# Writing out the loop over the six layers on every engine

## The chip, the cores and the metric

The kernel runs on one core of one Trainium2 chip. The metric is the time on the device of one execution, in microseconds (us), as the median of three runs. One more execution was recorded by the hardware profiler; its rows are in the section ahead of the prediction. TensorE is called PE in them (PEld is its weight load), VectorE DVE, ScalarE ACT, GpSimd POOL, SyncE SP.

## The reference, cut to what matters

Four blocks follow each other, each on the layer-normed stream, with the result added back: causal attention with 16 heads, a gated low-rank mixture of experts, chunked retention, and a transformer of six layers. The last is where the change is and where most of the time goes:

```
for layer in range(6):
    x = x + attn_layer(shift_tokens(x), Wqkv[layer], ...)   # 16 heads of 64, window 32, l2norm, rotary with scales
    x = x + ffn_layer(shift_tokens(x), W1[layer], ...)      # layer norm, 128 -> 2*341, a * gelu(gate), 341 -> 128
```

Here x has 16 sequences of 256 tokens of 128 numbers, all in float32.

## The kernel before

Each engine has a program of its own, and they meet in semaphores. The function `layers` holds the six layers. On each engine `one_layer(layer)` issues one layer, and a hardware loop runs it six times with `layer` in a register, for instance `with pe.Fori(0, DEPTH) as layer` (line 1259; 1013 on POOL, 1402 on DVE, 1542 on ACT, 930 on SP). So each engine has the code of one layer once and branches back to its head five times.

Within a layer there are two parts.

**The window attention** is a software pipeline over 16 sequences x 4 steps (two tiles of 128 tokens, two halves of the heads). `pipeline` writes out the four steps of sequence 0, runs sequences 1 to 14 in an inner hardware loop of 14 passes (line 899), and writes out sequence 15 and four steps of draining. A step on PE is, in this order: project keys (L1095), turn queries (L1103), project queries (L1095), turn keys (L1103), turn probabilities (L1128), values (L1115), scores (L1173, 64 small matmul passes), values (L1115), apply probabilities (L1154, some 28 small ones). ACT squares the projections (L1450, L1458), DVE rotates them (L1320), POOL adds (L979) and scales (L995) the rotated halves, and PE turns them in the next step.

**The MLP** goes over eight chunks of 512 tokens: the first are interleaved with the draining steps, then comes an inner hardware loop (line 911) of three passes with two chunks each, and the last chunk is written out. L1074 is the up projection, L1083 the down projection, ACT's L1425 the gelu, DVE's L1302 the product and L1309 the addition to the stream.

The end of a layer already does work for the next: SP has loaded the next attention weights, PE fuses them (L1025), ACT and DVE take the fused weights (L1410, L1271), DVE makes the rotation tables (L1265). Then the head of the next layer begins: on PE with waits on the fused weights and on the shifted tokens `w_xs` (ACT L1432), and with `project(1)`, L1095.

Waits are on counts that grow over the whole run, such as `passed(layer * N + seq * STEPS + ...)`. Where `layer` or `seq` is a register, register instructions work the count out ahead of the wait.

Of the kernel before, what the change touches and what calls it, by code (L numbers as in the profile page):

```python
# [40 lines left out]
DEPTH, WH, WD, WIN = 6, 16, 64, 32  # L41
# [26 lines left out]
def passed(count):  # L68
    return count + 1
# [772 lines left out]
def layers(nc, sem, sb, h, xT, spare0, spare1, banks, ident, wqk, wv, wo, base, scl, tab, mask, w1, w2, col):  # L842
# [64 lines left out]
    def finished(layer, c):  # L907
        return passed(layer * NCH + NCH + c)
# [18 lines left out]
    with nc.Block() as block:  # L927
        @block.sync
        def _(sp):
            with sp.Fori(0, DEPTH) as layer:  # L930
                sp.wait_ge(M["residual"], finished(layer, 0))
                sp.sem_inc(sem("gate"), 1)
                sp.wait_ge(S["u_made"], passed(layer * N * 2 + N))
                sp.sem_inc(sem("gate"), 1)
                for dst, name in ((w1, "m_w1"), (w2, "m_w2"), (col, "m_col")):
                    sp.dma_start(dst[:], h[name][bass.ds(layer, 1)].squeeze(0)).then_inc(S["mlp_weights"], 16)
                sp.wait_ge(S["u_made"], passed((layer + 1) * N * 2))
                sp.sem_inc(sem("gate"), 1)
                sp.wait_ge(S["tabled"], passed(layer + 1))
                sp.sem_inc(sem("gate"), 1)  # L940
                sp.wait_ge(M["residual"], finished(layer, 2))
                sp.sem_inc(sem("gate"), 1)
                load_window_weights(sp, S["weights"], h, (layer + 1) % DEPTH, wqk, wv, wo, scl)

        @block.gpsimd
        def _(pool):
# [63 lines left out]
                        shift_chunk(i * 2 + k, k)  # L1010
                        invert(i * 2 + k)

            with pool.Fori(0, DEPTH) as layer:
                one_layer(layer)

        @block.tensor
        def _(pe):
            def fuse(turn, part):
                for par in range(2):
                    if part == 1:  # L1020
                        pe.wait_ge(S["fused_taken0"], passed(turn * 2 + par + 1))
                        pe.sem_inc(sem("gate"), 1)
                    rows = slice(64 * par, 64 * par + 64)
                    for g in range(NPAIR):
                        last = nc.tensor.matmul(fused_bank(par)[:, g], wv[rows, part * NPAIR + g, :],  # L1025
                                                wo[rows, part * NPAIR + g, :], start=True, stop=True)
                    last.then_inc(S["fused"], 1)
# [228 lines left out]
            pe.wait_ge(S["weights"], 64)  # L1256
            fuse(0, 0)
            fuse(0, 1)
            with pe.Fori(0, DEPTH) as layer:
                one_layer(layer)  # L1260

        @block.vector
        def _(dve):
# [4 lines left out]
            def take_fused(turn):  # L1268
                for par in range(2):
                    dve.wait_ge(S["fused"], passed(turn * 4 + 2 + par + 1))  # L1270
                    nc.vector.tensor_copy(fused_weights(par, 1), fused_bank(par)).then_inc(S["fused_taken1"], 1)  # L1271
# [127 lines left out]
            dve.wait_ge(S["weights"], 64)  # L1399
            tables()  # L1400
            take_fused(0)
            with dve.Fori(0, DEPTH) as layer:
                one_layer(layer)

        @block.scalar
        def _(act):
            def take_fused(turn):
                for par in range(2):
                    act.wait_ge(S["fused"], passed(turn * 4 + par + 1))
                    nc.scalar.activation(fused_weights(par, 0), fused_bank(par), ACT.Copy).then_inc(S["fused_taken0"], 1)  # L1410
# [128 lines left out]
                gelu(NCH - 1, 1, 2)  # L1539

            take_fused(0)
            with act.Fori(0, DEPTH) as layer:
                one_layer(layer)


def load_window_weights(sp, weights, h, layer, wqk, wv, wo, scl):

    def of(name):
        return h[name][bass.ds(layer, 1)] if not isinstance(layer, int) else h[name][layer:layer + 1]
    sp.dma_start(wqk[:], of("w_qk").squeeze(0)).then_inc(weights, 16)  # L1550
    sp.dma_start(wv[:], of("w_v").squeeze(0)).then_inc(weights, 16)
    sp.dma_start(wo[:], of("w_o").squeeze(0)).then_inc(weights, 16)
    sp.dma_start(scl[:], of("w_scl").broadcast_to([P, 2 * WD])).then_inc(weights, 16)
# [83 lines left out]
```

## Time and profile before

| | us |
|---|---|
| median of three runs | 3930.85 |
| lowest and highest of them | 3927.55, 3932.21 |
| the profiled execution's own time | 3925.54 |
| its span in the profile | 3923.7 |
| PE busy | 3752.4 (96%) |
| DVE busy | 3199.5 (82%) |
| ACT busy | 2779.9 (71%) |
| POOL busy | 2574.1 (66%) |

PE is marked busy nearly all the time. Matmuls are pipelined, so this says that PE had work nearly all the time, and not that it ran at its peak. The profiled execution took 5.3 us less than the median of the runs, which is about as much as the runs differ among themselves. The span starts with the first instruction; between it and the execution's own time lie 1.8 us.

### The profile page before, as it was taken

What the parts mean: (1) busy time and instruction counts of PE and PEld (TensorE: products, weight loads), DVE (VectorE), ACT (ScalarE), POOL (GpSimd) and SP (SyncE); (2) the same over time, 40 slices, a digit from 0 to 9 for tenths busy, and PEclk for the clock granted to TensorE, in tenths of its full rate; (3) what the DMA queues carried; (4) which work ended last, traced back from release to release, by engine and by line L of the source; (5) the groups of instructions that cost most, each with busy time, mean ns of one, the idle gap of its engine ahead of it and who ended that gap; (6) DMA issues with size and microseconds to landing.
All of it is one profiled execution on the core that took longest, in us unless ns stands there. A gap on an engine that the chain in (4) does not pass through costs nothing. (4 is left out here: it accounts for less than half of the span.)

```text
span 3923.7 us, 156108 instructions
## 1 busy us (share of the span) xinstructions
PE 3752.4 (96%) x61563; PEld 2392.6 (61%) x61579; DVE 3199.5 (82%) x5483; ACT 2779.9 (71%) x6389; POOL 2574.1 (66%) x2467
## 2 busy tenths in 40 slices
PE   7997898999999999999999999999999999999998
PEld 4665684666655666646666556666466665566664
DVE  6886556899967999868999779999589997699996
ACT  6984215888846888748888568887388885588883
POOL 4553334788836888737888458887278885488882
PEclk9999998999999999999999999999999999999999
DMA  2000000000000000000000000000000000000001
GB/s 77 0 0 1 1 0 1 1 5 0 0 23 3 0 5 0 1 24 1 0 5 0 23 3 0 5 0 1 24 1 0 5 0 23 3 0 5 0 1 44
DMA packets 12428, 28.26 MB, mean 7 GB/s; under 512 B 2460, under 2 KB 6728, under 8 KB 11344
## 3 DMA queue, kind: packets, MB, share of 16 engines
q1 hardware_dynamic: 12240, 25.72, 1.9%
q8 instruction: 122, 2.00, 0.2%
q14 instruction: 66, 0.54, 0.0%
HBM read 23.62 MB, written 2.10 MB: 7 GB/s over the span
## 5 line engine op out<-in xcount | busy, mean ns | idle before, releaser
L979 POOL TENSOR_TENSOR w_t<-w_t 128x512 f32<-128x512 f32 x768 | 979.4, 1285 | 413.5 <-DVE w_t L1320 413.5
L1320 DVE TENSOR_TENSOR w_t<-banks,w_tab 128x512 f32<-128x512 f32 x1536 | 956.0, 684 | 237.7 <-ACT w_sq L1450 228.9
L995 POOL TENSOR_TENSOR w_t<-w_t,w_rn 128x512 f32<-128x512 f32 x768 | 784.4, 1042 | 251.7 <-ACT w_rn L1492 251.7
L1095 PE MATMUL banks<-w_qk,w_xs 128*128 128x512 f32 x1536 | 826.2, 620 | 10.5 <-issue 9.4
L1115 PE MATMUL banks<-w_vo,w_xs 128*32 128x256 f32 x12288 | 823.3, 385 | 4.9 <-ACT w_us L1443 4.9
L1103 PEld LDWEIGHTS banks<-ident,w_t 128*128 128x128 f32 x3072 | 380.2, 140 | 424.1 <-issue 405.0
L1443 ACT ACTIVATE w_us<-banks 128x512 f32<-128x512 f32 x768 | 456.8, 595 | 162.4 <-PE banks L1115 157.8
L1103 PE MATMUL banks<-ident,w_t 128*128 128x128 f32 x3072 | 461.1, 273 | 18.6 <-POOL w_t L995 10.5
L1115 PEld LDWEIGHTS banks<-w_vo,w_xs 128*32 128x32 f32 x12288 | 321.8, 109 | 243.5 <-issue 78.0
L1360 DVE TENSOR_REDUCE w_ss<-w_sq 128x16 f32<-128x1024 f32 x384 | 465.0, 1211 | 0.0
L1154 PE MATMUL banks<-w_us,w_prT 128*32 128x128 f32 x10752 | 410.5, 273 | 22.4 <-issue 17.7
L1002 POOL TENSOR_TENSOR w_pr<-w_pr,w_rl 128x512 f32<-128x512 f32 x384 | 402.4, 1048 | 34.0 <-ACT w_rl L1497 34.0
L1173 PEld LDWEIGHTS banks<-w_kT,w_qT 64*32 64x32 f32 x24576 | 319.1, 105 | 156.6 <-issue 156.6
L1154 PEld LDWEIGHTS banks<-w_us,w_prT 128*32 128x32 f32 x10752 | 349.7, 110 | 92.3 <-issue 31.4
L1173 PE MATMUL banks<-w_kT,w_qT 64*32 64x64 f32 x24576 | 381.2, 219 | 0.0
L1450 ACT ACTIVATE w_sq<-banks 128x512 f32<-128x512 f32 x384 | 229.3, 597 | 192.6 <-PE banks L1095 183.6
L1338 DVE TENSOR_TENSOR w_pr<-banks,w_mx 128x256 f32<-128x256 f32 x768 | 290.4, 420 | 21.0
L1364 DVE TENSOR_REDUCE w_tot<-w_pr 128x8 f32<-128x512 f32 x384 | 263.4, 686 | 37.7 <-ACT w_pr L1473 17.7
L1095 PEld LDWEIGHTS banks<-w_qk,w_xs 128*128 128x128 f32 x1536 | 231.3, 190 | 97.5 <-issue 97.5
L1458 ACT ACTIVATE w_sq<-banks 128x512 f32<-128x512 f32 x384 | 229.7, 598 | 83.2 <-PE banks L1095 83.2
L1425 ACT ACTIVATE logv<-banks,m_col 114x512 f32<-114x512 f32 x144 | 98.9, 687 | 265.8 <-PE banks L1074 265.8
L1074 PE MATMUL banks<-logv,m_w 128*114 128x512 f32 x576 | 271.0, 605 | 6.8 <-ACT logv L1418 6.8
(178 smaller groups left out, 6051.1 us busy)
## 6 DMA issues: line engine op xcount, KB each, us to landing
w_qk<-w_qk_in SPq DMA_DIRECT2D x7, 1024.0 KB, 4.8
w_v<-w_v_in SPq DMA_DIRECT2D x7, 512.0 KB, 5.6
w_o<-w_o_in SPq DMA_DIRECT2D x7, 512.0 KB, 6.4
m_w<-m_w_in SPq DMA_DIRECT2D x6, 342.0 KB
xT<-x_in SPq DMA_DIRECT2D x4, 512.0 KB, 5.7
out<-kept SPq DMA_DIRECT2D x8, 256.0 KB, 2.4
m_w<-m_w_in SPq DMA_DIRECT2D x6, 171.0 KB
r_tab<-r_tab_in SPq DMA_DIRECT2D x1, 512.0 KB
```

The costliest lines, as they stand in the source:

```text
L979: nc.gpsimd.tensor_tensor(v1, v1, v2[:, :, ::-1, :], ALU.add).then_inc(S["added"], 1)
L995: nc.gpsimd.tensor_tensor(v1, v1, rn[j % 2][:, i * HALF:(i + 1) * HALF].unsqueeze(2) .broadcast_to([P, HALF, WD]), ALU.mult).then_inc(S["n ...
L1002: nc.gpsimd.tensor_tensor(p[:], p[:], rl[j % 2][:].unsqueeze(1).unsqueeze(3) .broadcast_to([P, 2, HALF, WIN]), ALU.mult).then_inc(S["weigh ...
L1095: nc.tensor.matmul(banks[:, i, :], x[:], wqk[:, i * INNER + hh * C:i * INNER + (hh + 1) * C], start=True, stop=True).then_inc(S["qk"], 1)
L1103: last = nc.tensor.transpose(banks[:, 3 + i, g * P:(g + 1) * P], t1[j1 % 2][:, lo:lo + P], ident[:])
L1115: last = nc.tensor.matmul(banks[WIN * g:WIN * (g + 1), 2, lo:lo + 2 * P], x[:, WIN * w:WIN * (w + 1)], wvo[:, first:first + 2, :].rearrang ...
L1154: last = nc.tensor.matmul(banks[WIN * w:WIN * (w + 1), 7, 0:P], prT[:, chunk, WIN * w:WIN * (w + 1)], rhs, start=(hv == 0 and i == 0), sto ...
L1173: last = nc.tensor.matmul(bank[WIN * w:WIN * (w + 1), g], qT[j1 % 2][rows, g, WIN * w:WIN * (w + 1)], kT[rows, hk * NPAIR + g, lo:lo + 2 * ...
L1320: nc.vector.tensor_tensor(dst[j % 2][:, i * C:(i + 1) * C].rearrange("p (h d) -> p h d", d=WD), src, tab[:, 2 * t + cs, i * WD:(i + 1) * W ...
L1338: nc.vector.tensor_tensor(pr[j2 % 2][:, :, par * NPAIR:(par + 1) * NPAIR].rearrange("p a g r -> p g a r"), heads[:, par], mx[j2 % 2][:, pa ...
L1360: nc.vector.tensor_reduce(ss[j % 2][:], sq[:].rearrange("p a h d -> p (a h) d"), AX, ALU.add)\
L1443: nc.scalar.activation(us[j][:, 2 * a:2 * a + 2].rearrange("p w a n -> p (w a n)"), banks[:, 2, :], ACT.Copy).then_inc(S["u_taken"], 1)
```

## The change

On all five engines the hardware loop over the layers becomes a loop in the language that writes the program. Each engine then has the code of all six layers one behind the other; there is no branch back to a layer's head, `layer` is a constant, and the counts that depend on it alone are constants too. The inner loops at lines 899, 911 and 1008 stay hardware loops. The work on each engine and its order are the same.

```diff
@@ -927,7 +927,7 @@
         @block.sync
         def _(sp):
-            with sp.Fori(0, DEPTH) as layer:
+            for layer in range(DEPTH):
                 sp.wait_ge(M["residual"], finished(layer, 0))
@@ -1256,7 +1256,7 @@
             fuse(0, 0)
             fuse(0, 1)
-            with pe.Fori(0, DEPTH) as layer:
+            for layer in range(DEPTH):
                 one_layer(layer)
```

The same line changes in the same way on POOL, DVE and ACT. In the built program PE grows from 2711 to 8872 instructions, ACT from 735 to 2026, DVE from 745 to 1996, POOL from 363 to 1002, SP from 205 to 248 (a float32 matmul counts once here, and is two passes with a weight load each on the chip).

On PE this is the end of a layer's code before the change, from the second down projection of the last chunks to the branch back:

```order
L1079 REGISTER_ALU
L1083 MATMUL banks<-norm,m_w 128x512
L1081 REGISTER_ALU
L1083 MATMUL banks<-norm,m_w 128x512
L1081 REGISTER_ALU
L1083 MATMUL banks<-norm,m_w 128x512
L1259 REGISTER_ALU
L1259 COMPARE_AND_BRANCH
```

And this is the head of a layer's code on PE before the change, to which that branch goes back (`w_qk` and `w_vo` are the weights, `w_xs` the shifted tokens):

```order
L1259 ISA
L1187 ISA
L1095 MATMUL banks<-w_qk,w_xs 128x512 x2
L1115 MATMUL banks<-w_vo,w_xs 32x256 x8
L1109 ISA
L1115 MATMUL banks<-w_vo,w_xs 32x256 x8
L1182 ISA
```

With the change, the end of layer 0 and the head of layer 1 stand behind each other on PE:

```order
L1083 MATMUL banks<-norm,m_w 128x512 x3
L1025 MATMUL banks<-w_o,w_v 128x128 x8
L1083 MATMUL banks<-norm,m_w 128x512 x3
L1095 MATMUL banks<-w_qk,w_xs 128x512 x2
L1115 MATMUL banks<-w_vo,w_xs 32x256 x16
L1095 MATMUL banks<-w_qk,w_xs 128x512
L1103 MATMUL banks<-ident,w_t 128x128 x4
```

The last down projections (L1083) are followed at once by the first projection (L1095), and the branch and the register instructions around it are gone.

On ACT this is the end of a layer's code before the change, and behind the line of dots the head to which it branches:

```order
L1422 REGISTER_ALU
L1424 REGISTER_ALU
L1425 ACTIVATE logv<-banks,m_col 114x512
L1542 REGISTER_ALU
L1542 COMPARE_AND_BRANCH
...
L1414 ACT_TABLE_LOAD
L1525 ISA
L1432 ACTIVATE w_xs<-xT 64x128 x2
```

And the same place on ACT with the change:

```order
L1410 ACTIVATE w_vo<-banks 128x4x128 x2
L1425 ACTIVATE logv<-banks,m_col 114x512
L1414 ACT_TABLE_LOAD
L1432 ACTIVATE w_xs<-xT 64x128 x2
L1450 ACTIVATE w_sq<-banks 128x512
```

The last gelu is followed at once by the table load of the next layer. In the inner loops the streams are nearly what they were: on PE the code of the loop at line 899 has 383 instructions before and 381 (layer 0) or 383 with the change, on ACT 96 and 96, on DVE 62 and 62, on POOL 38 and 38 or 39.

## Rows read from the trace of the kernel before

**Rows 1.** The page's head and its busy times by engine.

```profile
span 3923.7 us, 156108 instructions
PE 3752.4 (96%) x61563; PEld 2392.6 (61%) x61579; DVE 3199.5 (82%) x5483; ACT 2779.9 (71%) x6389; POOL 2574.1 (66%) x2467
```

**Rows 2.** Windows: stretch, length, busy by engine, clock, DMA.

```profile
1260.00:1600.00 340.00, 340.00 (x6837) 221.46 (x6836) 309.04 (x504) 282.78 (x694) 274.68 (x264) 1.00 0.01 2
1123.00:1175.00 52.00, 51.15 (x184) 24.35 (x178) 32.91 (x102) 16.18 (x25) 11.88 (x16) 1.00 0.12 42
1193.00:1221.00 28.00, 23.80 (x394) 12.64 (x395) 21.40 (x33) 18.94 (x45) 19.30 (x19) 1.00 0.01 3
```

**Rows 3.** Waits of PE over the whole span: total, times, longest.

```profile
PE banks L1154 <- issue: 19.2, 20, 1.8
...
PE banks L1095 <- issue: 9.4, 5, 2.0
...
PE banks L1103 <- issue: 8.0, 6, 1.6
```

**Rows 4.** Timeline around the start of layer 1: start, length, what, idle before.

```profile
1187.92 1.28 DVE L1271 COPY w_vo<-banks 128x512 f32<-128x512 f32 x2
1188.03 0.64 ACT L1432 ACTIVATE w_xs<-xT 64x128 f32<-64x128 f32 x2
1188.19 2.84 PE L1083 MATMUL banks<-norm,m_w 114*128 114x512 f32 x6
...
1191.07 0.75 DVE L1309 SCALAR_TENSOR_TENSOR xT<-banks,m_col,xT 128x512 f32<-128x512 f32 x1 [1.86 <-PE banks L1083]
...
1192.86 1.95 PE L1095 MATMUL banks<-w_qk,w_xs 128*128 128x512 f32 x4 [1.83 <-issue]
...
1194.00 0.60 ACT L1450 ACTIVATE w_sq<-banks 128x512 f32<-128x512 f32 x1 [5.33 <-PE banks L1095]
1194.62 2.48 DVE L1320 TENSOR_TENSOR w_t<-banks,w_tab 128x512 f32<-128x512 f32 x4 [2.81 <-ACT w_sq L1450]
```

**Rows 5.** The page's DMA queues: packets, bytes, share of 16 engines.

```profile
q8 instruction: 122, 2.00, 0.2%
q14 instruction: 66, 0.54, 0.0%
```

**Rows 6.** DMA queues at the start of layer 1, from 1187 to 1194.

```profile
q8 instruction: 3, 0.05, 4.5%
q14 instruction: 3, 0.02, 1.1%
```

**Rows 7.** The only queue with packets from 1260 to 1610, in the inner loop.

```profile
q1 hardware_dynamic: 408, 0.53, 0.5%
```

**Rows 8.** Windows: first and second pass of layer 1's loop.

```profile
1221.40:1249.80 28.40, 26.87 (x549) 17.38 (x551) 24.03 (x41) 22.77 (x54) 21.28 (x21) 1.00 0.01 3
1249.80:1278.30 28.50, 28.50 (x582) 18.59 (x577) 25.87 (x44) 23.69 (x60) 22.99 (x22) 1.00 0.00 0
```

**Rows 9.** Timeline of PE: layer 0's draining steps, then layer 1's first pass.

```profile
1106.71 0.85 PE L1154 MATMUL banks<-w_us,w_prT 128*32 128x128 f32 x19
1109.26 0.63 PE L1154 MATMUL banks<-w_us,w_prT 128*32 128x128 f32 x9 [1.70 <-issue]
...
1233.80 0.51 PE L1154 MATMUL banks<-w_us,w_prT 128*32 128x128 f32 x11
1234.75 0.27 PE L1154 MATMUL banks<-w_edge,w_prT 128*32 128x128 f32 x1 [0.45 <-issue]
...
1239.34 0.99 PE L1173 MATMUL banks<-w_kT,w_qT 64*32 64x64 f32 x64
1240.26 1.07 PE L1115 MATMUL banks<-w_vo,w_xs 128*32 128x256 f32 x16
1242.41 0.43 PE L1154 MATMUL banks<-w_us,w_prT 128*32 128x128 f32 x8 [1.08 <-issue]
```

**Rows 10.** Timeline of ACT across its own branch back.

```profile
1184.16 0.69 ACT L1425 ACTIVATE logv<-banks,m_col 114x512 f32<-114x512 f32 x1 [1.39 <-PE banks L1074]
1186.73 1.28 ACT L1414 ACT_TABLE_LOAD   x1 [1.89 <-issue]
```

More of the change, by code:

```diff
@@ L1011, in one_layer @@
                         invert(i * 2 + k)
-            with pool.Fori(0, DEPTH) as layer:
+            for layer in range(DEPTH):
                 one_layer(layer)
@@ L1258, in _ @@
             fuse(0, 1)
-            with pe.Fori(0, DEPTH) as layer:
+            for layer in range(DEPTH):
                 one_layer(layer)
@@ L1401, in _ @@
             take_fused(0)
-            with dve.Fori(0, DEPTH) as layer:
+            for layer in range(DEPTH):
                 one_layer(layer)
@@ L1541, in _ @@
             take_fused(0)
-            with act.Fori(0, DEPTH) as layer:
+            for layer in range(DEPTH):
                 one_layer(layer)
```

## The prediction

> **What bounds the kernel now.** I read the busy times first. PE is busy 3752.4 of 3923.7 us, and the other four engines are well below it [rows 1]. This is an average over stages, so the windows come next. In the inner loop of the attention PE is busy 340.00 of 340 us while DVE has 309.04 and ACT 282.78, and in the MLP it is busy 51.15 of 52 [rows 2]. The granted clock is 1.00 in both. At the head of a layer the picture is another one: from 1193 to 1221 PE has 23.80 of 28 us, since the pipeline is being filled [rows 2]. So PE sets the time in the long stretches, and the few places where it stands still count in full.
>
> The third view is PE's waits by line. The reader should look for idle time that ends with "issue", that is, with nothing that the profile shows. It has three entries that matter here: 9.4 us in 5 pieces before L1095, 19.2 us in 20 pieces before L1154, and 8.0 us in 6 pieces before L1103 [rows 3]. Five is the number of branches back to the head of a layer, and the timeline around one shows that the first entry is this branch. L1083 ends at 1188.19 + 2.84 = 1191.03 and L1095 begins at 1192.86, with 1.83 us of idle put down to issue [rows 4]. What L1095 needs was there long before: ACT's shifted tokens (L1432) end at 1188.03 + 0.64 = 1188.67, DVE's copy of the weights (L1271) at 1187.92 + 1.28 = 1189.20 [rows 4]. In the same seven microseconds the queues named "instruction" move 3 packets each [rows 6]. The page gives 122 packets and 2.00 MB for one of them, 16 KB each, and 66 packets and 0.54 MB for the other, 8 KB each [rows 5]. So code is fetched at the branch, in pieces, and PE stands until it is there. Inside the inner loop no such queue has a packet in 350 us [rows 7].
>
> **The change, part by part.**
>
> *The branch back on PE.* It goes, five times. With the change L1095 stands right behind the last L1083, and nothing that it waits for is later than 1189.20, so it can begin at about 1191.05 in place of 1192.86. Who follows must be able to follow. ACT's first square (L1450) has been idle for 5.33 us, waiting for L1095, and DVE's first rotation (L1320) for 2.81 us, waiting for that square. DVE's last work of the old layer, L1309, ends at 1191.07 + 0.75 = 1191.82, while its rotation would begin at 1194.62 - 1.8 = 1192.8 [rows 4]. So the whole chain moves forward, and the next thing to be late is L1309, 1.0 us away. I take the full idle time of the five: -9.4 us [rows 3]. Bounds: 0 if the same pieces are just as late without a branch, and -9.4 if all go; L1309 has room for it.
>
> [...]
>
> *The branches back on ACT and DVE.* ACT stands 1.89 us across its own branch before its table load at 1186.73 [rows 10]. The load ends at 1188.01, the shifted tokens at 1188.67, and PE comes to use them only at 1191.03. With the change they are done some 1.9 us earlier and wait. What hides it are PE's down projections, 2.84 us of them in the last row; had PE arrived before 1188.67, the 1.89 us would count. Price 0. DVE and POOL wait for PE and ACT there in the same way: 0. SP's program has nothing else around its branch: 0.
>
> *Register instructions.* On PE the address of each down projection was worked out by one (L1081), and counts by others; with a constant layer most go from the written-out parts. They run ahead of the array, and the array has work in 51.15 of 52 us where they are densest [rows 2], so their removal gives 0. Bounds: nothing can be lost by it, and at most the 0.85 us idle of such a 52 us window could come back, in part, in six layers; I put 0 to -2. In the inner loop PE has 381 or 383 instructions in place of 383, and ACT and DVE as many as before. POOL has one more, with 274.68 of 340 busy [rows 2]: 0.
>
> *Code that runs for the first time.* This is the term with the largest uncertainty. The code of a layer's attention is longer on PE than what is kept, so in each layer it is fetched anew, before and with the change: before because the branch went back, with the change because it is new code. In straight code the next piece is mostly there in time, but not always. The first pass of layer 1's loop has PE busy 26.87 of 28.40, the second 28.50 of 28.50 [rows 8]. The idle time of the first pass lies between matmuls of one line: 1.08 us before an L1154 at 1242.41, 0.45 at 1234.75, and 1.70 in the draining steps at 1109.26 [rows 9]. All are put down to issue. I read them as borders between two pieces that fall where the matmuls are shortest: nineteen matmuls take 0.85 us in L1154, while six take 2.84 us in L1083, so a piece of L1154 is used up sooner than the next arrives. Over the run these are the 19.2 us in 20 places [rows 3]. The size of a layer's code does not change by more than a few register instructions, so there are as many borders as before. But before, they fell on the same instructions in each of six layers; with the change each layer begins at another place within a piece. I counted where the borders fall: in stretches of short matmuls there would be about 33 in place of 42, but more of them in the densest part, and the six stalls of up to 1.8 us in the draining steps would mostly be gone. Weighted by the idle times of rows 9 both come to about 18 us. I take 0. Bounds: -19.2 if no border hurts any more; +19.2 if they hurt twice as much.
>
> *Sum.* -9.4 + 0 + 0 + 0 = -9.4 us, that is 3925.54 - 9.4 = 3916.1 for an execution like the profiled one (whose own time is its span of 3923.7 and 1.8 around it). That execution was 5.3 us under the median of the runs, 3930.85. Against the median the forecast is 3930.85 - 9.4 = 3921.5 us, 0.24% less. About 0.2% (7.9 us) is what a measurement of this kernel can tell from no change, so faster begins at 3923.0 and the forecast is just past it.
>
> **The rivals.**
>
> *The borders fall better.* If half of the 19.2 us goes too, the time is 3921.5 - 9.6 = 3912. For it: 33 borders in place of 42 in the short stretches, and the 1.70 us of the draining steps avoided. Against it: the others are in the worst stretch of a step, L1173 and L1154.
>
> *The borders fall worse.* Half as much again, +9.6 us, eats the gain: 3931. For it: the first pass would now be hit at other places in each layer, and a stall of 1.08 us is seen there already.
>
> *The change does not do what it says.* At the seam PE also needs a new piece of code. If it is loaded only when the last is used up, the gap before L1095 stays: 3930. Against it: the last piece before the seam holds the long L1083 (0.47 us each), the best cover that there is, and a straight border under long matmuls shows no idle in the window from 1123 to 1175 beyond 0.85 us [rows 2].
>
> *The inner loop of ACT is fetched again in every pass (the slower side).* The pieces of the other engines are half as large, and by their packets (66, for six times some 735 + 745 instructions and once 363 + 205) hold some 140 instructions each. ACT's inner loop has 96. Before, it began at one place in all six layers and no fetch was seen in it [rows 7]. With the change it begins at six different places, and by my count lies across a border in three layers. If a branch back over a border costs what the branch back to the head costs, 1.89 us [rows 10], then 3 x 14 passes x 1.89 = 79 us, of which ACT's slack of 340 - 282.78 in 340 us, 4.8 us a pass, hides a part that depends on how closely ACT is tied to PE: +20 to +79, about 3980 at the middle. It decides as soon as one such border is missed in each pass. Against it: a pass of PE's inner loop has 582 matmuls and 577 weight loads. An instruction takes some 57 bytes (0.54 MB for the same 9,450), so these are about four pieces of 16 KB, and they run with no fetch and no gap, 28.50 of 28.50 us [rows 5, 7, 8].
>
> [...]
>
> **How the numbers follow.** Chances: the forecast 0.50, borders better 0.20, borders worse 0.15, the gap stays 0.08, the loop fetched again 0.07. The predicted time is that of the first, 3921.5. Its own spread is about 5 us either way, from the borders, the 0 to -2 of the registers, and the spread of the medians (3927.55 to 3932.21). The range goes down to 3911, which takes in nearly all of the second case, and up to 3932, which takes in the fourth and most of the third; the fifth is left out, as are the ends of the two border cases, together 2 in 10. Faster by over 0.2% (below 3923.0): 0.36 of the first case and the second, 0.56. Within it: 0.14 of the first, 0.14 of the third and all of the fourth, 0.36. Slower (above 3938.7): the fifth and 0.01 of the third, 0.08.
>
> **What would show it right or wrong.** In the profile of the changed kernel the entry of L1095 with issue should be gone or near nothing, and at each layer's start L1095 should follow L1083 within 0.2 us. L1154 with issue should be near 19 us, but at changing places; its total against 19.2 decides between the three border cases. An inner pass from the second on should take 28.5 us in every layer with no instruction packets; if a layer's passes are longer and such packets come with each, it is the last rival. The number of packets of both instruction queues should be about what it was, 122 and 66. What would make the forecast wrong is first of all the border term, which is twice as large as the gain and rests on a count.

## The result and the profile after

The changed kernel takes 3901.46 us (median of 4 runs, 3900.35 to 3905.15), the kernel before 3930.34 us (median of 4, 3927.55 to 3932.21). The ratio is 0.993, with an interval of 0.9914 to 0.9945. The gain is 28.9 us, three times what was forecast, and it lies outside the range, which went down to 3911. The profiled execution of the changed kernel has a span of 3898.6 us, 25.1 less than that of before [rows 1]. The accounts below are made between these two spans.

The page's head, busy times and instruction queues of the changed kernel, which answer to [rows 1, 5]:

```profile
span 3898.6 us, 154887 instructions
PE 3742.7 (96%) x61579; PEld 2391.6 (61%) x61579; DVE 3204.7 (82%) x5483; ACT 2778.7 (71%) x6389; POOL 2574.7 (66%) x2467
q8 instruction: 108, 1.77, 0.2%
q14 instruction: 41, 0.34, 0.0%
```

PE is busy 9.7 us less than before with the same matmuls. That part isn't idle time: the matmuls themselves took less time somewhere. The granted clock accounts for it. Within the layers of before it is 0.50 for 20.4 us in all (1110.7 to 1117.5, 1656.9 to 1663.7, 2284.9 to 2288.3 and 3291.9 to 3295.3), and in the changed kernel it is 1.00 from the first layer's L1095 to 3892.

PE's waits over the whole span after the change (total, times, longest), to be read against [rows 3]:

```profile
PE banks L1103 <- issue: 10.5, 10, 1.7
PE banks L1154 <- ACT w_prT L1468: 7.8, 6, 1.3
PE banks L1154 <- issue: 6.1, 8, 1.1
```

The entry of L1095 with issue, 9.4 us in 5 pieces before, is down to 0.2 us in one piece. L1154 with issue went from 19.2 us in 20 pieces to 6.1 in 8. In the kernel before the wait of L1154 for ACT was this:

```profile
PE banks L1154 <- ACT w_prT L1468: 3.1, 6, 0.8
```

So 4.7 us of the 13.1 came back as a wait for ACT, which the idle for code had hidden.

The start of layer 1 after the change, in the timeline (start, length, what, idle before), to be read against [rows 4]:

```profile
1184.63 1.88 PE L1083 MATMUL banks<-norm,m_w 114*128 114x512 f32 x4
1186.34 1.88 PE L1095 MATMUL banks<-w_qk,w_xs 128*128 128x512 f32 x4
1186.55 0.75 DVE L1309 SCALAR_TENSOR_TENSOR xT<-banks,m_col,xT 128x512 f32<-128x512 f32 x1 [1.86 <-PE banks L1083]
1187.40 0.60 ACT L1450 ACTIVATE w_sq<-banks 128x512 f32<-128x512 f32 x1 [5.21 <-PE banks L1095]
1188.10 2.48 DVE L1320 TENSOR_TENSOR w_t<-banks,w_tab 128x512 f32<-128x512 f32 x4 [0.81 <-ACT w_sq L1450]
```

L1095 follows L1083 without idle, and DVE's L1320 stands 0.8 us behind L1309, as the forecast had it (1.0).

The first two passes of layer 1's inner loop and the first stretch of its steady state after the change (stretch, length, busy by engine, clock, DMA), to be read against [rows 2, 8]:

```profile
1250.00:1600.00 350.00, 350.00 (x7019) 228.03 (x7012) 317.82 (x519) 291.21 (x717) 282.66 (x271) 1.00 0.01 2
1214.30:1242.70 28.40, 27.52 (x541) 17.80 (x543) 24.06 (x41) 22.39 (x53) 21.68 (x21) 1.00 0.01 3
1243.10:1271.60 28.50, 28.50 (x582) 18.59 (x578) 25.88 (x44) 23.68 (x59) 23.01 (x22) 1.00 0.00 0
```

The steady state is what it was. The last rival (ACT's loop fetched again in each pass) has nothing for it: from 1250 to 1600 only one queue has packets, and it isn't one for instructions.

```profile
q1 hardware_dynamic: 408, 0.53, 0.5%
```

**Where the 25.1 us lie.** Both traces have 61579 weight loads on PE, so the n-th of one is the n-th of the other, and the start times can be subtracted place by place. The table below is made in this way, for all runs. Its columns are sums over the six layers, in us: the head of a layer (from the last L1083 to the last step before the inner loop), the loop's first pass, its other 13 passes, the draining steps with the first MLP chunks, the MLP loop, and the whole from the first L1095 to the last L1083. (The last chunks of each layer, behind the MLP loop, have no column; they are about 86 us in all, before and after.)

| | head | first pass | passes 2-14 | draining | MLP loop | whole |
|---|---|---|---|---|---|---|
| before | 206.1 | 180.6 | 2187.9 | 293.8 | 313.2 | 3267.9 |
| after | 196.2 | 177.1 | 2188.0 | 284.8 | 311.0 | 3243.3 |
| e1 PE alone | 209.1 | 176.9 | 2188.3 | 284.6 | 311.0 | 3256.2 |
| e2 all but PE | 209.6 | 180.7 | 2187.8 | 289.0 | 313.2 | 3266.6 |
| e3 three layers a pass | 204.9 | 177.8 | 2188.4 | 285.7 | 312.5 | 3255.6 |
| e4 before, moved by 160 | 207.8 | 175.1 | 2188.4 | 280.9 | 312.2 | 3250.7 |
| e5 PE and DVE | 195.9 | 177.0 | 2188.1 | 284.0 | 311.0 | 3242.2 |
| e6 before, hints | 199.0 | 181.9 | 2188.4 | 300.1 | 312.3 | 3268.0 |
| e7 after, loop at 175 | 199.7 | 180.0 | 2189.1 | 284.3 | 311.0 | 3250.3 |
| e8 after, loop at 80 | 202.5 | 174.8 | 2189.1 | 282.2 | 311.0 | 3246.1 |
| e9 after, head at 32 | 197.5 | 174.9 | 2187.9 | 281.3 | 311.0 | 3238.9 |
| e10 after, head at 155 | 195.6 | 180.5 | 2187.7 | 298.6 | 311.1 | 3259.9 |
| e11 before, hints, head at 14 | 202.4 | 175.3 | 2188.0 | 280.9 | 312.3 | 3245.1 |

The first L1095 starts at 645.8 us in the kernel before and at 645.2 in the changed one; that is the 0.6 missing to 25.1. (It varies from 645.2 to 648.7 between runs whose code ahead of it is the same, so a part of each difference in time is from there.) The head gave 10.0 us, which is the term of the branch. The rest, 14.6 us, is the draining steps (9.0), the first pass (3.5) and the MLP loop (2.2). The forecast had 0 to -2 there.

### The profile page after: what moved, and what is told of

The parts are those of the page before. It is cut to its first block and busy times, and to the rows that moved or that the text cites. A ratio compares the mean times of both kernels' runs of the same rounds, so it can differ in the third digit from the quotient of the medians.

```text
span 3898.6 us, 154887 instructions
## 1 busy us (share of the span) xinstructions
PE 3742.7 (96%) x61579; PEld 2391.6 (61%) x61579; DVE 3204.7 (82%) x5483; ACT 2778.7 (71%) x6389; POOL 2574.7 (66%) x2467
## 5 line engine op out<-in xcount | busy, mean ns | idle before, releaser
L1320 DVE TENSOR_TENSOR w_t<-banks,w_tab 128x512 f32<-128x512 f32 x1536 | 959.0, 685 | 225.7 <-ACT w_sq L1450 215.7
L1115 PE MATMUL banks<-w_vo,w_xs 128*32 128x256 f32 x12288 | 823.1, 385 | 4.9 <-ACT w_us L1443 4.9
L1095 PE MATMUL banks<-w_qk,w_xs 128*128 128x512 f32 x1536 | 825.8, 620 | 1.1 <-DVE w_vo L1271 0.8
L1103 PEld LDWEIGHTS banks<-ident,w_t 128*128 128x128 f32 x3072 | 380.2, 140 | 429.0 <-issue 409.7
L1103 PE MATMUL banks<-ident,w_t 128*128 128x128 f32 x3072 | 461.5, 273 | 22.5 <-POOL w_t L995 12.0
L1115 PEld LDWEIGHTS banks<-w_vo,w_xs 128*32 128x32 f32 x12288 | 321.6, 109 | 242.7 <-issue 77.0
L1154 PE MATMUL banks<-w_us,w_prT 128*32 128x128 f32 x10752 | 409.7, 273 | 12.9 <-ACT w_prT L1468 7.8
L1173 PEld LDWEIGHTS banks<-w_kT,w_qT 64*32 64x32 f32 x24576 | 319.4, 106 | 157.4 <-issue 157.4
L1154 PEld LDWEIGHTS banks<-w_us,w_prT 128*32 128x32 f32 x10752 | 350.8, 110 | 80.0 <-issue 17.0
L1173 PE MATMUL banks<-w_kT,w_qT 64*32 64x64 f32 x24576 | 381.6, 219 | 0.7 <-issue 0.7
L1095 PEld LDWEIGHTS banks<-w_qk,w_xs 128*128 128x128 f32 x1536 | 231.8, 190 | 86.1 <-issue 86.1
L1332 DVE TENSOR_REDUCE w_mx<-banks 128x8 f32<-128x512 f32 x384 | 265.6, 692 | 13.0
```

Source lines behind the costliest of these rows:

```text
L1095: nc.tensor.matmul(banks[:, i, :], x[:], wqk[:, i * INNER + hh * C:i * INNER + (hh + 1) * C], start=True, stop=True).then_inc(S["qk"], 1)
L1103: last = nc.tensor.transpose(banks[:, 3 + i, g * P:(g + 1) * P], t1[j1 % 2][:, lo:lo + P], ident[:])
L1115: last = nc.tensor.matmul(banks[WIN * g:WIN * (g + 1), 2, lo:lo + 2 * P], x[:, WIN * w:WIN * (w + 1)], wvo[:, first:first + 2, :].rearrang ...
L1154: last = nc.tensor.matmul(banks[WIN * w:WIN * (w + 1), 7, 0:P], prT[:, chunk, WIN * w:WIN * (w + 1)], rhs, start=(hv == 0 and i == 0), sto ...
L1173: last = nc.tensor.matmul(bank[WIN * w:WIN * (w + 1), g], qT[j1 % 2][rows, g, WIN * w:WIN * (w + 1)], kT[rows, hk * NPAIR + g, lo:lo + 2 * ...
L1320: nc.vector.tensor_tensor(dst[j % 2][:, i * C:(i + 1) * C].rearrange("p (h d) -> p h d", d=WD), src, tab[:, 2 * t + cs, i * WD:(i + 1) * W ...
```

## The experiments

### Which engine's loop

The first two write the loop out on a part of the engines. For e1 only the line on PE is changed:

```diff
-            with pe.Fori(0, DEPTH) as layer:
+            for layer in range(DEPTH):
                 one_layer(layer)
```

> The loop over the layers is written out on PE alone; SP, POOL, ACT and DVE keep their hardware loops. Theory A (all of the gain is PE's own: its branch back, its code borders, its register instructions): the same as with all five engines written out, 3901 us within 3, that is 0.9926 of before, and the layer heads without idle before L1095. Theory B (part of the gain is from ACT and DVE, whose branches back cost 1.9 us each, or from POOL): it stays at 3905 to 3911.

For e2 the same line is changed on SP, POOL, DVE and ACT, and PE keeps its loop.

> The loop is written out on SP, POOL, ACT and DVE, and PE keeps its hardware loop: the complement of the run on PE alone. Theory A: no change, 3930 us within 4, with the same five idles before L1095 and the same 19 us before L1154. Theory B: 3920 to 3926.

e1 takes 3915.97 us, ratio 0.9965 (0.9951 to 0.9979). e2 takes 3928.02, ratio 0.9999 (0.999 to 1.0009). PE alone gives 11.5 us, the others alone nothing, all together 28.9. The two parts don't add up, and neither theory gave 3916. (In the profile of e2 the heads are 3.5 us longer than before and the draining steps 4.8 shorter. The granted clock, of which more below, was 0.50 for 3.4 us behind four of the five seams, that is, the places where one layer ends and the next begins, and in one draining part; in the profile of before this was so behind one seam and in three draining parts.) The timeline of e1 at the start of layer 1 shows what is between them:

```profile
1189.49 1.88 PE L1095 MATMUL banks<-w_qk,w_xs 128*128 128x512 f32 x4
1189.69 0.75 DVE L1309 SCALAR_TENSOR_TENSOR xT<-banks,m_col,xT 128x512 f32<-128x512 f32 x1 [1.86 <-PE banks L1083]
1190.55 0.60 ACT L1450 ACTIVATE w_sq<-banks 128x512 f32<-128x512 f32 x1 [3.04 <-PE banks L1095]
...
1192.84 2.48 DVE L1320 TENSOR_TENSOR w_t<-banks,w_tab 128x512 f32<-128x512 f32 x4 [2.39 <-issue]
...
1198.59 0.63 PE L1103 MATMUL banks<-ident,w_t 128*128 128x128 f32 x4 [3.23 <-issue]
...
1199.06 1.85 PE L1095 MATMUL banks<-w_qk,w_xs 128*128 128x512 f32 x2
```

PE starts L1095 at once, and ACT's square is done at 1191.15. But DVE stands 2.39 us behind its last L1309, with issue (2.29 to 2.53 at the five seams): this is DVE's own branch back. The kernel before has the same code on DVE. There the square came late as well, because of PE's 1.83 us, so the profile put DVE's idle time of 2.81 us down to ACT and showed nothing of the branch [rows 4]. PE then stands 3.23 us before L1103, where it stood 1.7 in the changed kernel, and the matmuls behind that idle are slow: the granted clock is 0.50 from 1199.1 to 1202.5, and in the last row a pair of L1095 takes 1.85 us, where four of them take 1.88 in the first row. So the head of e1 is even 3.0 us longer than before (209.1 against 206.1), and its gain is all from other places.

e5 has the loop written out on PE and DVE, with the two changed lines of the kind shown.

> The loop is written out on PE and DVE; SP, POOL and ACT keep their hardware loops. Theory A2 (the branches back of PE and of DVE lie beside each other, 1.8 and 2.4 us of idle, so taking one away shows only the other; those of ACT, POOL and SP are covered): all of the gain is back, 3901 us within 3, the fill of the pipeline 32.1 us in layers 1 to 5 where PE alone had 34.5 to 35.4, and no idle with issue before DVE's L1320. Theory B2 (ACT's branch or POOL's is part of it): 3904 to 3914, with the fill at 33 us or more.

It takes 3902.21 us, ratio 0.9936 (0.992 to 0.9953), within a microsecond of the changed kernel. Filling the pipeline at the start of layers 1 to 5 takes 32.1, 32.1, 32.1, 32.4 and 32.1 us, against 34.5 to 35.4 in e1. The loops of ACT, POOL and SP are worth nothing. Theory A2 holds. The branches of PE and DVE lie beside each other, and only taking away both gives the 10 us.

### Registers or borders

e3 keeps layer in a register on PE, with two passes of three layers, and moves two of three copies to other places in the code pieces:

```diff
-            with pe.Fori(0, DEPTH) as layer:
-                one_layer(layer)
+            with pe.Fori(0, DEPTH // 3) as half:
+                for k in range(3):
+                    one_layer(half * 3 + k)
```

> On PE alone the hardware loop makes two passes with three layers written out in each, so that layer stays a register (every register instruction stays) and four of the five branches back go. The copies of a layer start at three different places within a code piece. Theory A (branch and borders): seams without a branch take 2.0 us less each, the one with a branch as before; the draining steps are shorter in layers 1, 2, 4 and 5, where the border is no longer at their L1154, and as before in layers 0 and 3; the three passes of the MLP loop stay at 52.2 us, where the changed kernel has 51.8. In all 3911 us. Theory C (the gain beyond the branch comes from the register instructions that constants save): only the seams get shorter, 3922 us.

The time is 3920.74 us, 0.9981 (0.9971 to 0.999), where theory A had 3911 and theory C 3922. By the time alone theory C would have it. DVE's branch takes the seams' gain here as in e1, which theory A had not reckoned with, and the ten executions are far apart: 3912.82 to 3926.51. The profiled one is the fastest of them, with no low clock in any draining part. Its layers tell the rest. The second part of the draining steps takes 26.0, 25.2, 25.1, 26.1, 25.1 and 25.1 us: shorter in just the four layers whose code was moved, with all register instructions in place. The MLP loop takes 52.0 us in the moved copies with registers, where it takes 52.2 before and 51.8 with constants. So the registers are worth 0.2 us a layer, 1.2 in all, and theory C falls.

e4 is the kernel before, with its loops, and 160 instructions ahead of PE's loop over the layers:

```diff
+            for _ in range(160):
+                pe.sem_inc(sem("gate"), 1)
             pe.wait_ge(S["weights"], 64)
             fuse(0, 0)
             fuse(0, 1)
             with pe.Fori(0, DEPTH) as layer:
```

> The kernel before with 160 semaphore increments on PE ahead of the loop over the layers, and nothing else changed; they lie in the wait for the block to begin, or cost some us once. All of PE's layer code moves by 160 instructions within the code pieces. Theory A: by count the borders then fall into L1173 and L1115 rather than L1154; idle with issue before L1154 falls from 19.2 to under 6 us, the draining steps (28.4, 28.4, 26.7, 26.4, 27.6, 26.4 us in the six layers) take 25.2 us in each, and the kernel takes 3930 - 17 = 3913 us though the branch is still there. Theory C: no change, 3930 us, plus what the increments cost.

It takes 3937.05 us, 1.0021 (1.0012 to 1.0031), where theory A had 3913. The increments cost far more than I had thought: the first L1095 starts at 670.9 us, 25.1 us later than before, about 0.16 us for each increment.

```profile
PE banks L1025 <- issue: 31.9, 1, 31.9
PE banks L1103 <- issue: 15.2, 12, 2.8
...
PE banks L1154 <- ACT w_prT L1470: 7.5, 6, 1.3
```

Behind that one cost the layers are 17.2 us shorter (3250.7 against 3267.9), as theory A had said, though nothing in them was changed. The second part of the draining steps takes 25.14 or 25.15 us in each layer, and L1154 with issue is down to 0.4 us in one piece. Where the borders between code pieces fall is worth this much by itself.

The trace of before ties this idle time to code directly. The queue q8 is PE's: it has 108 packets in e1 and 122 in e2, where q14 has 66 and 41. Each of the 20 idle times before L1154 that end with issue ends 2.4 to 2.8 us after a packet of the queue q8, "instruction", begins. For instance, the one that ends at 1109.26 [rows 9] follows a packet that begins at 1106.61 and has landed at 1107.82. In the changed kernel the 8 that are left end 2.35 to 2.6 us after such a packet.

### The place, set on purpose

The language can set a place within a code piece for an instruction. In the traces PE's code of layers 1 to 4 of the changed kernel is 15,766 instructions, each counted once, and 61 packets of q8 fall on it, 258 to a packet; all counts of places here take a piece as 256. e7 and e8 set the place of the head of PE's inner loop in the changed kernel, to 175 and 80:

```diff
-        with eng.Fori(1, B - 1) as seq:
+        slot = {"engines": [eng.engine], "head_slot": {eng.engine: 175}} if eng.engine == nc.tensor.engine else {"engines": [eng.engine]}
+        with nc.Fori(1, B - 1, **slot) as seq:
```

> The changed kernel, with the head of PE's inner loop set in each layer to the place within a code piece of 256 instructions that it has in the kernel before (175, by count); the engine jumps over the gap, which costs 6 taken branches. Theory D (where borders fall sets the rest of the gain): the first pass takes 30 us and idle with issue before L1154 is back at 15 to 20 us, the draining steps take 26 to 28.4 us, and the time rises by 7 to 14 us to about 3911. Theory E (what counts is that the code is new, or the registers): 3903 us, with the draining steps at 25.2 us.

> The same with the head at 80 in each layer, near where layer 2 of the changed kernel and the kernel before with 160 increments had it, both without idle before L1154. Theory D: idle with issue before L1154 under 2 us, first pass 29.0, draining steps 21.65 and 25.15 us in every layer: 5.4 us less than the changed kernel, and some 2 us for the jumps: 3898 us. Theory E: 3903 us.

The profiles show a jump over the gap ahead of the loop's head: both have 154893 instructions, six more than the changed kernel's 154887, and the six are branches on PE at the line of the loop (90 in place of 84). They take 0.19 to 0.32 us in e7 and 1.32 to 1.72 us in e8.

e7 takes 3908.21 us, 0.9949 (0.9932 to 0.9965), e8 3905.43, 0.9943 (0.9927 to 0.996). e7 is between its two theories (3911 and 3903), and e8 is above both of its own (3898 and 3903), so by their times they decide nothing. The first passes came as expected (30.0 and 29.1 us a layer), and neither the draining steps of e7 nor the jumps did. L1154 with issue is 7.2 us in e7, where 15 to 20 was expected, and 0.6 in e8. With constants the draining steps have 27 instructions fewer on the way to the L1154 in question, so by count the border fell on L1074, and the steps took 284.3 us, no more than after. And a jump right ahead of L1095 costs 0.9 to 1.3 us in e8 (six idle times with issue; 0.39 to 0.41 us in five layers of e7), which used up its gain.

e9 and e10 set the place of the head of each layer instead, where PE's queue is ahead of the array (in layers 1 to 5 of both the jump begins 3.7 us ahead of the start of the L1095 that follows):

```diff
             for layer in range(DEPTH):
+                pe.addr_align(256, offset=32, max_nops=0)
                 one_layer(layer)
```

> The changed kernel with the head of each layer's code on PE set to place 32 of a code piece; the gap is jumped over ahead of the first L1095, where PE's queue is some us ahead of the array. The inner loop then begins near 80, as in the run that set the loop's own head, but without its 1.1 us before L1095 in each layer. Theory D (borders): no idle before L1154 or the first L1095, first pass 29.1 us, draining steps 21.65 and 25.15: 7 us less than the changed kernel, 3895 us. Theory F (the jump waits for a new piece wherever it stands, for there is no prefetch across it): about 1.1 us or more before each L1095 at a layer's start, 3900 to 3903 us.

> The same with the head at 155. By the count of instructions a border then falls on the L1154 of the draining steps on which it fell in the kernel before (setting the inner loop to its old place did not do that, since the written-out draining steps have 27 instructions fewer on the way). Theory D with the clock: the 1.7 us of idle are back at that L1154 in all layers, in some layers the granted clock falls to 0.50 for the 4 us behind it as it did in three layers before, the draining steps (second part) take 26.3 us without the fall and 28.4 with it, in place of 25.2, and the time is 3910 to 3918 us. Theory E (it is not the border): as the other alignment, within 2 us.

e9 takes 3897.95 us (3896.93 to 3899.07), 0.992 (0.9904 to 0.9937). e10 takes 3917.46 (3914.81 to 3923.28), 0.9973 (0.9962 to 0.9983). The two differ in one number of the program, and in 19.5 us. PE's waits of e9:

```profile
PE banks L1103 <- issue: 11.1, 12, 1.7
...
PE banks L1095 <- issue: 1.9, 6, 0.3
...
PE banks L1154 <- issue: 0.8, 2, 0.6
```

and of e10:

```profile
PE banks L1154 <- issue: 14.5, 17, 2.1
...
PE banks L1103 <- issue: 9.5, 6, 1.7
```

Theory D holds in both directions (3895 and 3910 to 3918 were expected). Theory F falls: in layers 1 to 5 of e9 the jump takes 0.40 to 3.20 us, and no idle time stands before the first L1095 behind it. (The six of 0.3 us in the rows of e9 stand behind the inner loop's first pass, as six such do in e8. e9 has one new idle time of 1.3 us before an L1115, in the head of layer 2.) The timeline of e10 in layer 0's draining steps reads like that of the kernel before [rows 9], and shows in addition what follows the idle time:

```profile
1109.45 0.85 PE L1154 MATMUL banks<-w_us,w_prT 128*32 128x128 f32 x20
1111.98 0.60 PE L1154 MATMUL banks<-w_us,w_prT 128*32 128x128 f32 x8 [1.67 <-issue]
1112.51 0.66 PE L1062 MATMUL banks<-ident,logv 128*128 128x128 f32 x4
1114.29 3.73 PE L1074 MATMUL banks<-logv,m_w 128*114 128x512 f32 x4 [1.13 <-ACT logv L1419]
```

Four L1074 take 3.73 us. In the changed kernel the same four take 1.94:

```profile
1109.00 1.94 PE L1074 MATMUL banks<-logv,m_w 128*114 128x512 f32 x4 [1.13 <-ACT logv L1418]
```

The windows of e10 over this place in layers 0 to 3 show the granted clock in the third column from the end:

```profile
1114.40:1118.00 3.60, 3.60 (x5) 1.37 (x6) 0.69 (x1) 2.02 (x4) 1.05 (x1) 0.50 0.00 0
1660.00:1664.00 4.00, 3.19 (x47) 1.94 (x45) 2.69 (x13) 1.84 (x3) 2.02 (x3) 1.00 0.02 4
2199.60:2203.20 3.60, 3.60 (x5) 1.36 (x6) 0.69 (x1) 2.08 (x4) 1.05 (x1) 0.50 0.00 0
2745.30:2748.80 3.50, 3.50 (x7) 1.50 (x8) 0.69 (x2) 2.03 (x4) 1.05 (x1) 0.58 0.00 0
```

and so do those of the kernel before, in layers 0, 1, 2 and 4:

```profile
1111.61:1115.34 3.73, 3.73 (x5) 1.48 (x6) 0.69 (x1) 2.13 (x4) 1.05 (x1) 0.50 0.02 4
1657.87:1661.40 3.53, 3.53 (x5) 1.30 (x6) 0.69 (x1) 2.02 (x4) 1.05 (x1) 0.50 0.02 5
2205.00:2208.60 3.60, 2.80 (x37) 1.74 (x39) 1.96 (x10) 2.87 (x5) 1.05 (x1) 1.00 0.02 5
3292.00:3295.40 3.40, 3.40 (x5) 1.20 (x6) 0.69 (x1) 1.97 (x4) 1.05 (x1) 0.52 0.02 5
```

Two idle times stand close together here, 1.7 us for code and 1.13 us for ACT's L1418, and in some layers the clock falls to 0.50 for 3.4 or 6.8 us, and in others it doesn't. Mostly it falls with the second of them; in e2 (layer 3), e6 (layers 0 and 1) and e10 (layer 3) it fell before the second began, so the first alone was enough. With the first of the two gone it is at 1.00 in all layers of the changed kernel, of e5, e9 and e11. That is not a rule: in e7 (layers 0, 1 and 4) and e8 (layer 0) the clock fell for 3.4 us behind smaller ones, 0.4 to 0.7 us for code before L1062 and 1.13 to 1.48 before L1074. The changed kernel has 0.67 and 1.13 us there in layer 0, and the clock did not fall. Where the idle time before L1154 is 1.4 to 2.1 us, it fell in 15 of 26 layers (before, e2, e3, e6 and e10). What decides in the single case stays open.

### The same without writing the loop out

e6 is the kernel before with a hint on two branches:

```diff
-            with pe.Fori(0, DEPTH) as layer:
+            with nc.Fori(0, DEPTH, engines=[pe.engine], hint_back_edge=True) as layer:
...
-            with dve.Fori(0, DEPTH) as layer:
+            with nc.Fori(0, DEPTH, engines=[dve.engine], hint_back_edge=True) as layer:
```

> The kernel before with its hardware loops on all engines; on PE and DVE the branch back to the layer's head is announced to the engine by a prefetch hint at the head of each pass. Theory A2: the seams lose their idle of 1.8 us before L1095 and nothing else changes (draining steps 26.4 to 28.4 us, 19 us before L1154), 10 us less than before, 3918 us. If the hint does nothing here: 3928 us. Theory C (the gain is in the registers): 3928 us as well.

It takes 3923.14 us, 0.9986 (0.9977 to 0.9996), where 3918 was expected. In its timeline L1095 has 0.58 us of idle time in place of 1.83 (0.34 to 0.65 at the five seams):

```profile
1191.83 2.84 PE L1083 MATMUL banks<-norm,m_w 114*128 114x512 f32 x6
...
1195.25 1.96 PE L1095 MATMUL banks<-w_qk,w_xs 128*128 128x512 f32 x4 [0.58 <-issue]
```

Its heads are 7.1 us shorter. The profiled execution, 3927.98 us and so 4.8 above the median, has the low clock in the draining steps of all six layers (28.3 to 28.7 us for the second part in five of them, 27.6 in one), so that its whole is as long as before. e11 adds the place:

```diff
-            with nc.Fori(0, DEPTH, engines=[pe.engine], hint_back_edge=True) as layer:
+            with nc.Fori(0, DEPTH, engines=[pe.engine], hint_back_edge=True, head_slot={pe.engine: 14}) as layer:
```

> The kernel before with its hardware loops, the hints on PE's and DVE's branch back, and the head of PE's loop over the layers at place 14 of a code piece, so that the inner loop begins near 80. Theories A2 and D together: the seams are 1.3 us shorter as with the hints alone (-7 us), and the borders leave the draining steps' L1154 (-17 us with the clock's part): 3905 us, most of what writing out the loop gives, with a ninth of its PE code in place. If the two effects are one and the same, or overlap: 3913 us or more.

(PE's program is a third as long as the changed one, 2711 against 8872 instructions, and not a ninth.) It takes 3904.87 us (3904.05 to 3906.81), 0.994 (0.9923 to 0.9956), as forecast. The whole is 22.8 us shorter than before with every loop in place.

## Why the prediction was wrong

*The branch back on PE, -9.4 us: right in size, in part by luck.* The heads gave 10.0 us. The step that followed the chain past PE said that DVE's L1309 was next to be late, 1.0 us away. It overlooked that behind L1309 DVE had its own branch back, 2.39 us. This was priced at 0 with ACT's, because "DVE and POOL wait for PE and ACT there in the same way". That is true only while PE is late; e1 took away PE's branch alone and the head got longer by 3.0 us. The sum held because the change happens to take both branches away, and not because the second one had been seen. ACT's, POOL's and SP's at 0 was right (e5).

*Register instructions, 0 with -2 as a bound: within the bound.* It is -1.2 us, all in the MLP loop (e3). They have an effect of another kind, though: with some 27 instructions fewer ahead of it, the L1154 of the draining steps stands at another place within a code piece. That this is why e7 did not bring the idle time back is by count.

*Code that runs for the first time, 0: this step failed.* It was put at 0 and came to about -13.4 us: 3.5 in the first passes, 9.0 in the draining steps, and 1.0 of the MLP loop (its 2.2 less the 1.2 of the registers), with 0.1 the other way in passes 2 to 14. The reading of rows 9 was right: the border on L1154 was the cause of the 1.70 us in the draining steps and of the idle time in the first pass, as e4, e9 and e10 and the times of the instruction packets show. The direction of the draining steps was foreseen as well. Two things in the weighing were wrong.

First, the 33 borders in short stretches were weighed as if L1173 were as bad as L1154 ("the worst stretch of a step"), which made up for the six that went. By count, the kernel before has borders in L1173 too (two in the draining steps' first part, one in the first pass), and no idle stands there. By the same count, in e9 and e4 nearly all borders of these stretches fall in L1173 and L1115, and L1154 with issue is 0.8 and 0.4 us. After the change 8 idle times before L1154 were left, 6.1 us, and not 18. A border there isn't always free: the changed kernel has 0.7 us once before L1173, e1 has 0.9 once, and e11 has 3.4 us in 6 pieces before L1115. Why it mostly costs less than one in L1154, right behind it, no run here tells.

Second, no price was set on the low clock that came behind such an idle time (in 15 of the 26 layers above). In three of the six layers of the profiled execution of before, the second part of the draining steps takes 28.4, 28.4 and 27.6 us, in the others 26.7, 26.4 and 26.4: 4.9 us for the clock, out of the 13.4. The idle time before L1154 is 13.1 us less, and 4.7 of that came back as the wait of L1154 for ACT. The three together make 13.1 + 4.9 - 4.7 = 13.3.

The same clock is the likeliest cause of the gap between 25.1 us by the two spans and 28.9 by the medians. The kernels that keep the idle time in the draining steps, in all layers or some, spread widely: before 3922 to 3932 over its 54 executions, e2 3924 to 3930, e3 3913 to 3927, e6 3918 to 3929, e10 3915 to 3923. Those without spread by 2 to 5 us (after, e5, e7, e8, e9, e11; e4 by 5). In the profiles the low clock was there in the draining steps of 1 of 6 layers (e2), 3 (before, e7), 5 (e10) and 6 (e6). The mean granted clock of each execution points the same way. Of the 50 of before that were run beside the experiments, the 14 at 0.987 took 3928.7 to 3932.0 us, and the 12 at 0.989 took 3922.8 to 3927.7. The ten of e3 go from 3912.82 at 0.991 to 3926.51 at 0.986, and the four of the changed kernel are at 0.991 or 0.992. The profiled execution of before is at 0.9895, above most others of its kernel. So the slower executions of before spent more time at the lower level; in which layers, only profiles would tell.

Of the rivals, "the borders fall better" came true with a larger effect than it was given: half of 19.2 us was expected to go, 13.1 went (4.7 of it into another wait), and the clock came on top. It had been given 0.20. The one on the slower side, ACT's inner loop fetched in each pass, had no sign for it: passes 2 to 14 take 2188.0 us after and 2187.9 before.

Of the signs, the idle time before L1095, the distance from L1083 and the inner pass of 28.5 us came as written. The number of instruction packets did not: it should have stayed at about 122 and 66 and is 108 and 41. On PE's queue q8 a layer has 15 or 16 packets, where layers 1 to 4 of before have 18.

Most borders cost nothing that shows: before has 105 packets on q8 in its six layers, and PE has 37 idle times with issue in them. But e9 and e10 differ only in the place of the six layer heads, and so in where all borders behind them fall, and are 19.5 us apart. In straight code the 1.83 us before L1095 are gone; with the hint of e6 0.58 us are left there.

## What to carry to other kernels

Where a kernel's time moves though none of its work did, look for idle time with issue between matmuls of one line, and at the granted clock right behind it. In a body whose code is fetched again in each pass (15 to 18 packets a layer on PE here), the place of its head within a code piece was worth up to 19.5 us of 3900, more than the branch. Before an edit to one engine's loop is priced, look at what the other engines do at the same branch, since two waits beside each other can show as one, with only the last named: DVE's 2.81 us here were all put down to ACT. Here e9 (loop written out, head of each layer set to place 32) was the fastest, 3897.95 us; its layers are 4.4 us shorter than those of the changed kernel, and the medians, taken at different times, 3.5 us. e11 gives most of it with every loop kept.

## What the runs showed of the hardware that was not expected

- One idle time of 1.4 to 2.1 us, with another of 1.13 us behind it, went with a granted clock of 0.50 for 3.4 or 6.8 us in some layers and not in others (before, e2, e6, e10): four L1074 took 3.73 us in place of 1.94.
- The idle times before L1154 that end with issue end 2.4 to 2.8 us after an instruction packet of PE's queue begins (all 20 in before).
- A semaphore increment on PE took about 0.16 us where nothing else went on (e4: the layers began 25.1 us later for 160 of them; that start varies by up to 3.5 us by itself).
- A jump over a gap in the code left 0.9 to 1.3 us of idle time before L1095 ahead of the inner loop in e8, and 0.39 to 0.41 us in five layers of e7. At the heads of layers 1 to 5 it left none there (e9, e10), where it began 3.7 us ahead of the start of L1095.
- A branch back that was announced by a hint left 0.34 to 0.65 us of idle time before L1095 at the five seams (e6), in place of 1.8 to 2.0.
- PE's inner loop has some 1,200 instructions a pass as they run (1140 weight loads and matmuls, 73 of the sequencer), 4.7 pieces at 256 to a piece (258 instructions to a packet in the changed kernel), and was run 14 times in each layer of before with no packet on q8 from its second pass on.
